# A state-space layer inside a four-layer kernel: two of its channel blocks convolved in the weights, its decay stage folded into its neighbours, and its decay rows made by one 32-row product a tile

## The reference

```python
zxbcdt = hn @ in_proj_w.T                      # (T, 644): z 256, xBC 384, dt 4
z, xBC = zxbcdt[:, :256], zxbcdt[:, 256:640]
dt = softplus(zxbcdt[:, 640:] + dt_bias)       # 4 heads
conv = conv_b + sum(pad(xBC)[k:k+T] * conv_w[:, k] for k in range(4))
x, B, Cc = split(silu(conv), (256, 64, 64))    # x: 4 heads of 64
dA = exp(dt * -exp(A_log))
state = state * dA_t + (dt_t * x_t) B_t        # per head, 64x64, over t
y_t = state C_t + D * x_t
out = rmsnorm(y * silu(z)) @ out_proj_w.T + residual
```

## Time and profile before

| | us |
|---|---|
| median of 3 runs | 5289.64 (5287.33 to 5296.65) |
| the profiled execution, its own time | 5287.22 |
| its span, first to last instruction | 5285.5 |
| outside the span | 1.7 |

### The profile page before, as it was taken

How to read it: one execution, slowest core, us unless ns; L and a number is a source line. 1 busy time by engine, 2 the same in 40 slices (tenths; PEclk the granted TensorE clock), 3 DMA queues, 4 the chain that set the end, 5 groups by cost and what they waited for, 6 DMA issues and landing times. The chain is left out here.

```text
span 5285.5 us, 74271 instructions
## 1 busy us (share of the span) xinstructions
PE 4229.8 (80%) x26784; PEld 2472.8 (47%) x26784; DVE 2894.0 (55%) x6283; ACT 2191.7 (41%) x4860; POOL 720.1 (14%) x780
## 2 busy tenths in 40 slices
PE   6787896798679789678777969968877786896887
PEld 3443234566444333456644433345664543334566
DVE  5554674454555476445455547644546554764454
ACT  3344464233334446323333544632333354463233
POOL 1100120310110112032011011203201101120320
PEclk8898897698789889779878988976987797897698
DMA  3101100100210111011021011101102101110110
GB/s 99 44 19 40 41 18 23 49 17 17 69 44 19 42 38 30 11 48 25 13 73 36 19 47 33 34 7 48 25 13 74 35 19 44 36 33 8 48 25 13
DMA packets 112338, 181.84 MB, mean 34 GB/s; under 512 B 25296, under 2 KB 63440, under 8 KB 109136
## 3 DMA queue, kind: packets, MB, share of 16 engines
q1 hardware_dynamic: 94480, 155.35, 10.7%
q10 hardware_dynamic: 17472, 21.51, 1.7%
HBM read 114.78 MB, written 27.26 MB: 27 GB/s over the span
## 5 line engine op out<-in xcount | busy, mean ns | idle before, releaser
L813 DVE TENSOR_REDUCE mhalf<-mx 128x1 f32<-128x512 f32 (+3 forms) x2064 | 1277.2, 654 | 734.6 <-PE mx L764 394.8
L786 ACT ACTIVATE prob<-ps_st 128x512 f32<-128x512 f32 (+3 forms) x2432 | 1116.9, 512 | 1296.9 <-PE ps_st L731 704.6
L761 PE MATMUL mx<-ks,qs 72*128 72x512 bf16 (+3 forms) x2304 | 847.1, 384 | 252.8 <-DVE mhalf L813 88.0
L728 PE MATMUL ps_st<-qs,ks 75*128 75x512 bf16 (+3 forms) x2432 | 751.8, 349 | 47.2 <-DMA qs<-neg 20.1
L761 PEld LDWEIGHTS mx<-ks,qs 72*128 72x128 bf16 x2304 | 233.7, 102 | 825.3 <-DVE mhalf L813 563.9
L711 PE MATMUL ps_o<-prob,vst 128*32 128x512 f32 (+3 forms) x5376 | 561.6, 501 | 0.3
L728 PEld LDWEIGHTS ps_st<-qs,ks 75*128 75x128 bf16 x2432 | 238.7, 100 | 273.4 <-ACT prob L786 142.5
L2241 ACT ACTIVATE pr<-ps,nm,lrq 128x192 f32<-128x192 f32 (+1 forms) x512 | 251.1, 502 | 239.3 <-DVE nm L2254 239.3
L2215 PE MATMUL po<-lv,ptr 128*128 128x64 f32 x1920 | 251.1, 285 | 5.6 <-DVE ptr L2266 5.6
L2215 PEld LDWEIGHTS po<-lv,ptr 128*128 128x128 f32 x1920 | 233.0, 198 | 37.2 <-DVE ptr L2266 30.2
L318 PE MATMUL turn<-table,nrm 128*128 128x128 f32 x224 | 63.6, 465 | 224.8 <-DVE nrm L297 224.8
(11 more groups left out here) (335 smaller groups left out, 7168.3 us busy)
## 6 DMA issues: line engine op xcount, KB each, us to landing
ks<-k_scr SPq DMA_DIRECT2D x144, 192.0 KB
qs<-q_scr SPq DMA_DIRECT2D x252, 96.0 KB
stream<-stream SPq DMA_DIRECT2D x16, 1152.0 KB, 9.8
k_scr<-ks SPq DMA_DIRECT2D x60, 192.0 KB
stream<-stream SPq DMA_DIRECT2D x16, 512.0 KB, 4.6
tabs<-local_tables SPq DMA_DIRECT2D x4, 2048.0 KB
lkt<-o SPq DMA_DIRECT2D x128, 64.0 KB, 2.1
lkt<-o ACTq DMA_DIRECT2D x128, 64.0 KB, 2.1
```

The lines of the kernel that those rows point to most:

```text
L728: last = nc.tensor.matmul(ps_st[:, u % 3, 0:q1 - q0], ks[g % 2][0:KR, h, kt * P:(kt + 1) * P], qs[g % 2][0:KR, hf, h, q0 - hf * HALF:q1 - ...
L761: last = nc.tensor.matmul(bank[:, j * w:(j + 1) * w], qs[g % 2][0:R, hf, h0 + j, (t - 4 * hf) * P:(t - 4 * hf + 1) * P], ks[g % 2][0:R, h0 ...
L786: nc.scalar.activation(prob[:, b % PROBS, h, 0:q1 - q0], ps_st[:, u % 3, 0:q1 - q0], ACT.Exp, scale=scale).then_inc(S["exped"], 1)
L813: nc.vector.tensor_reduce(mhalf[:, hf, h0:h0 + heads, t - 4 * hf, part], bank[:, 0:heads * (k1 - k0)].rearrange("p (n w) -> p n w", n=head ...
```

## The change

Nothing outside `mamba`, its packed weights and the constants changes. In the diff's order:

- The convolution of B and C (one block of 128 channels together) is put into the weights: POOL makes four scaled copies of their projection weights, one for each tap (wt), and PE accumulates four f32 products of 512 columns with shifted input columns for each half (`state_inputs`). ACT applies bias and silu straight from PSUM. C is moved to partitions 0 to 63 by a transfer. DVE convolves x's two halves only; the steps are interleaved with the small steps of dt.
- The phase m_decay is gone. Its sums are made on PE within m_proj, with one product more that gives the sums as 32 rows (4 heads of 8 tiles); DVE spreads these into a block-diagonal tile (`spread`). Its three small exponentials stand at the head of m_scan. xdt moves to POOL, one tile at a time; xw is made on DVE, one tile at a time, with dt folded into its weight.
- The decay rows of a tile are one f32 product of 32 rows and 512 columns and one bf16 mask product of 512 columns. DVE's subtraction is gone: ACT takes exp from PSUM with -cum as its bias, one instruction for each head. Decay rows are issued two tiles ahead.
- `keep_clock` issues products whose result nothing reads: three after each of the second half's four convolution steps, and ten between and behind the last turns of m_proj.

```diff
+    l3 += [("l3_cwr", np.concatenate([row(cw[256:, k]) for k in range(4)], 1)), ("l3_cbbc", cb[256:].reshape(-1, 1))]
...
+              ("own_tile", (q // 4 == np.arange(8)) * 1.0), ("own_head", (q % 4 == np.arange(4)) * 1.0),
...
+def keep_clock(net, bank, n):
+    for _ in range(n):
+        net.nc.tensor.matmul(bank, net.ident_bf, net.ident_bf.unsqueeze(1).broadcast_to([P, 4, P]), start=True, stop=True)
...
+                    sp.wait_ge(S["bc"], 2)
+                    sp.dma_start(c_ch[:, :], bc[N:P, :]).then_inc(S["c_moved"], 16)
...
+                    nc.gpsimd.tensor_tensor(wt[:, :, :], W("l3_xbc")[:, DI:DI + P].unsqueeze(1).broadcast_to([P, TAPS, P]),
+                                            W("l3_cwr").rearrange("p (k c) -> p k c", k=TAPS), ALU.mult).then_inc(S["taps"], 1)
...
+                    def state_inputs(i):
+                        pe.wait_ge(S["padded"], 3 + i)
+                        pe.wait_ge(S["taps"], 1)
+                        for k in reversed(range(TAPS)):
+                            a = max(0, TAPS - 1 - k - i * HALF)
+                            c0 = i * HALF + a - (TAPS - 1 - k)
+                            last = nc.tensor.matmul(pp[:, i, a:HALF], wt[:, k, :], net.in_ch[:, c0:c0 + HALF - a], start=(k == TAPS - 1),
+                                                    stop=(k == 0))
...
+                    pre(0)
+                    for t in range(NT):
+                        last = nc.tensor.matmul(p_dt[:, t, :], net.in_ch[:, t * P:(t + 1) * P], W("l3_dt"), start=True, stop=True)
+                    last.then_inc(S["dtmm"], 1)
+                    z(0)
+                    z(1)
+                    pre(1)
+                    z(2)
+                    z(3)
+                    for i in range(2):
+                        state_inputs(i)
+                    pe.wait_ge(S["step"], 9)
+                    flat = da[:, :, :].rearrange("p t h -> p (t h)")
+                    nc.tensor.matmul(pd[:, small:2 * small], net.K("tri"), flat, start=True, stop=True)
+                    nc.tensor.matmul(pd[:, 2 * small:3 * small], net.K("ones"), flat, start=True, stop=True)
+                    nc.tensor.matmul(p_rows, flat, net.K("tri"), start=True, stop=True).then_inc(S["cums"], 1)
+                    for t in range(4, NT):
+                        z(t)
+                    pe.wait_ge(S["bc"], 2)
+                    for i in range(2):
+                        turn(i, b_ch, N)
+                    for i in range(2):
+                        pe.wait_ge(S["silu"], i + 1)
+                        turn(2 + i, xs[:, 0, :], P)
+                    for k in range(5, 9):
+                        pe.wait_ge(S["conv"], k)
+                        keep_clock(net, spare[:, :], 3)
+                    for i in range(2):
+                        pe.wait_ge(S["silu"], 3 + i)
+                        turn(4 + i, xs[:, 1, :], P)
+                        keep_clock(net, spare[:, :], 2)
+                    keep_clock(net, spare[:, :], 4)
...
+                    nc.scalar.activation(na[:, :], W("l3_alog"), ACT.Exp).then_inc(S["nega"], 1)
+                    pads(0)
                     act.wait_ge(S["step"], 2)
                     nc.scalar.activation(e[:, :, :], e[:, :, :], ACT.Exp, scale=-1.0).then_inc(S["exp"], 1)
+                    pads(1)
                     act.wait_ge(S["step"], 3)
                     nc.scalar.activation(dt[:, :, :], v[:, :, :], ACT.Ln).then_inc(S["ln"], 1)
...
+                    conv(0, 3)
+                    conv(1, 0)
+                    conv(1, 1)
                     dve.wait_ge(S["cums"], 1)
+                    nc.vector.tensor_scalar(ncum[:, :, :], p_cum, -1.0, None, ALU.mult).then_inc(S["decay"], 1)
+                    nc.vector.tensor_copy(etot[:, :, :], p_tot).then_inc(S["decay"], 1)
+                    nc.vector.tensor_tensor(spread[:, :, :], p_rows.unsqueeze(1).broadcast_to([small, H, P]),
+                                            net.K("own_head")[0:small, :].unsqueeze(2).broadcast_to([small, H, P]), ALU.mult).then_inc(S["decay"], 1)
...
+                    conv(1, 2)
+                    for i in range(2):
+                        to_tok(i, b_tok[:, 4 * i:4 * i + 4, :], N)
+                    conv(1, 3)
...
+                    def inputs(t):
+                        nc.gpsimd.tensor_tensor(hd(xdt[:, t, :]), hd(x_tok[:, t, :]), wide(dt[:, t, :]), ALU.mult).then_inc(S["xdt"], 1)
...
-                        for h in range(H):
-                            nc.tensor.matmul(pr[:, t % 2, h, :], da[:, t, h:h + 1].broadcast_to([P, P]), net.K("tri"), start=True, stop=False)
-                            last = nc.tensor.matmul(pr[:, t % 2, h, :], net.ident_bf, net.later_kq, start=False, stop=True)
+                            pe.wait_ge(S["decay"], H * (t - 1))
+                        nc.tensor.matmul(pr[:, t % 2, :, :], net.K("own_tile")[0:NT * H, t:t + 1].broadcast_to([NT * H, P]), spread[:, :, :],
+                                         start=True, stop=False)
+                        nc.tensor.matmul(pr[:, t % 2, :, :], net.ident_bf, net.later_kq.unsqueeze(1).broadcast_to([P, H, P]), start=False,
+                                         stop=True).then_inc(S["rows"], 1)
...
+                        for h in range(H):
+                            nc.scalar.activation(ex[:, t % 2, h, :], pr[:, t % 2, h, :], ACT.Exp, bias=ncum[:, t, h:h + 1]).then_inc(S["decay"], 1)
...
+                    def weighted(t):
                         if t >= 2:
+                            dve.wait_ge(S["smm"], t - 1)
+                        nc.vector.tensor_tensor(hd(xw[:, t % 2, :]), hd(x_tok[:, t, :]), wide(wend[:, t, :]), ALU.mult).then_inc(S["xw"], 1)
```

More of the change, by code:

```diff
@@ L1559, in mamba @@
         da = kept("m_da", [P, NT, H])
-        with net.phase("m_proj", ["zero", "pre", "padded", "conv", "silu", "turned", "tok", "zmm", "z", "dtmm", "step", "exp", "ln", "nega"]) as (S, blk):
+        ncum = kept("m_ncum", [P, NT, H])
+        etot = kept("m_etot", [P, NT, H])
+        wend = kept("m_wend", [P, NT, H])
+        spread = kept("m_spread", [NT * H, H, P])
+        ss = kept("m_ss", [P, NT])
+        b_ch = bc[0:N, :]
+        with net.phase("m_proj", ["taps", "zero", "pre", "padded", "bcmm", "bc", "c_moved", "conv", "silu", "turned", "tok", "zmm", "z", "dtmm", "step",
+                                  "exp", "ln", "nega", "cums", "decay"]) as (S, blk):
             xp = net.tmp("xp", [P, 2, T + 3])
@@ L1571, in mamba @@
             pz = net.psum("pz", [P, 2, HALF])
[L1572 to L1588, removed]
+            pd = net.psum("pd", [P, HALF])
+            spare = net.psum("spare", [P, HALF])
+            small = NT * H
+            p_dt = pd[:, 0:small].rearrange("p (t h) -> p t h", h=H)
+            p_cum = pd[:, small:2 * small].rearrange("p (t h) -> p t h", h=H)
+            p_tot = pd[:, 2 * small:3 * small].rearrange("p (t h) -> p t h", h=H)
+            p_rows = pd[0:small, 3 * small:3 * small + P]
             with blk as block:
@@ L1608, in pre @@
+                            nc.tensor.matmul(pp[:, i, :], W("l3_xbc")[:, j * P:(j + 1) * P], net.in_ch[:, i * HALF:(i + 1) * HALF],
                                              start=True, stop=True).then_inc(S["pre"], 1)
[L1610 to L1620, removed]
@@ L1621, in _, with z @@
[L1621 to L1623 removed]
+                    def z(t):
+                        if t >= 4:
+                            pe.wait_ge(S["z"], t - 2 - t % 2)
+                        nc.tensor.matmul(pz[:, t // 2 % 2, t % 2 * DI:(t % 2 + 1) * DI], net.in_ch[:, t * P:(t + 1) * P],
+                                         W("l3_z"), start=True, stop=True).then_inc(S["zmm"], 1)
@@ L1624, in _, with turn @@
+                    def turn(k, src, m):
                         if k >= 2:
@@ L1651, in _ @@
-                    silu(act, 3)
+                    for t in range(4):
+                        gates(t)
+                    for i in range(2):
+                        act.wait_ge(S["bcmm"], i + 1)
+                        nc.scalar.activation(bc[:, i * HALF:(i + 1) * HALF], pp[:, i, :], ACT.Silu, bias=W("l3_cbbc")).then_inc(S["bc"], 1)
+                    silu(0)
+                    for t in range(4, NT):
+                        gates(t)
+                    silu(1)
                 @block.vector
@@ L1742, in mamba @@
-        with net.phase("m_scan", ["skip", "skipped", "gated", "sq", "rows", "diff", "decay", "gmm", "mt", "intra", "inter", "smm", "scaled", "state", "part", "y"]) as (S, blk):
+                    conv(0, 3)
+                    conv(1, 0)
+                    conv(1, 1)
+                    dve.wait_ge(S["cums"], 1)
+                    nc.vector.tensor_scalar(ncum[:, :, :], p_cum, -1.0, None, ALU.mult).then_inc(S["decay"], 1)
+                    nc.vector.tensor_copy(etot[:, :, :], p_tot).then_inc(S["decay"], 1)
@@ new lines, in _ @@
+                    conv(1, 3)
+                    for j in range(2):
```

(8 more changed lines are left out.)

188 lines of the change are left out of this document (82 added, 106 removed).

## The result

| | us |
|---|---|
| median before | 5293.15 (5287.33 to 5299.48, 4 runs) |
| median after | 5236.76 (5229.02 to 5250.91, 4 runs) |
| ratio | 0.9896, 95% interval 0.9871 to 0.9921 |
| profiled execution after, its own time and its span | 5229.02 and 5227.3 |

The change made the kernel faster, by 1.0%: 56 us, where 130 were forecast. The time lies in the range (5140 to 5265), which the rivals had widened, and 77 us from the predicted 5160: the forecast's own case did not happen.

A forecast was written before the change was run, and what follows sets the result against it. PE was taken to bound the scan. Per pass, scan -28.1, decay stage -6.9 and projection +2.5 gave -32.5; four passes -130, from 5287.2 to 5157, median 2.4 higher, so 5160 us; range 5140 to 5265.

The forecast's parts named there:

- the forecast's own case: Whole kernel: clock fast through the scan, 5160 us, own range 5140 to 5180, chance 0.48.
- the part on the clock: Scan: PE enters from unbroken keep_clock products, so the clock stays high through most of it; called the least certain step.
- The idle time ahead of the door: Change from projection to scan: PE idle some 0.7 us, after which the clock may be gone.
- The clock drops at the scan's door: Rival, scan start: clock lost at the 32-row products, scan 61 us, -7.5 a pass, 5260; chance 0.23.
- part of the way: Rival, scan: clock lost midway or in some passes; half the tiles at 7.25, -19.5 a pass, 5212; chance 0.22.
- The scan at 2.4 GHz: Scan: 4.0 us a tile, eight are 32, 4.0 for entry and tail, 36.0 against 64.1.
- DVE and POOL: Scan: they get in each other's way, DVE 3.15 to 4.15 us a tile, 0 to 1.2 us a scan.
- The main case's claim that PE stays the bound: Scan, per tile: DVE 2.55, ACT 2.1 and POOL 2.7 us all lie under PE's 4.0.
- The decay stage: m_decay, between projection and scan: gone as a phase, -6.9 us a pass.
- C's transfer: Projection: 256 KB starting near 21.5 us, needing less than 4.6, ending before 27 and costing nothing.
- The projection's +2.5: Projection: PE's order sums to 33.7 us against 31.2, +2.5 a pass; bounds 30 and 36.
- the twelve dummy products: Projection, keep_clock ahead of turn(4): 3.3 us with four starts, 2 to 3 us of the path.

The follow-up runs named there:

- e2: The changed kernel with the f32 decay product given 128 rows in place of 32, the added rows zeros; 5146.88 us, ratio 0.9729 to the kernel before.
- e5: The changed kernel with the f32 decay product given 64 rows in place of 32, the added rows zeros; 5147.1 us, ratio 0.9719 to the kernel before.
- e3: The changed kernel, 32 rows kept, plus three unread bf16 products of 128 rows and 384 columns in each tile's decay group; 5158.62 us, ratio 0.9766.
- e4: The changed kernel with the decay rows of the kernel before in place of the new ones, nothing else; 5146.17 us, ratio 0.9733.
- e8: The kernel before with keep_clock alone: ten products behind m_proj's last turn, twenty behind m_decay's sums; 5228.08 us, ratio 0.9881.
- e1: The changed kernel with all keep_clock products left out; 5235.05 us, ratio 0.9894 to the kernel before.
- e9: e5 with dt's products ahead of pre(0) on PE and dt's small steps ahead of convolution and copies; 5133.42 us, ratio 0.9708.
- e10: e5 (64 rows) without keep_clock; 5233.72 us, ratio 0.9905 to the kernel before.
- e7: e2 and e1 together: the changed kernel with 128 rows and no keep_clock; 5149.11 us, ratio 0.9723.
- e11: e7 (128 rows, no keep_clock) with dt's products first; 5202.85 us, ratio 0.9851 to the kernel before.

## Why the prediction was partly wrong

**The failed step** is in the part on the clock: "I take it that the clock stays high through most of the scan." It fell 2.5 us in, in three passes, and 11.5 us in, in one, and the scan took 60.2 and 52.8 us in place of 36.0. The cause is shown from both sides: it is the 32 rows of the decay product. Rows of zeros added to the same product (e2, e5) hold the clock; full-height work beside it (e3) holds it too, and the old rows (e4) do as well. The idle time ahead of the door, which the prediction named as a second suspect and put at 0.7 us, is 0.4 to 0.5 us in all of these. The prediction had priced 32 rows by their time and found no discount, which is right (1.09 us against 1.13), and noted that such products "stand in no row"; it did not let that decide the chances. Why few rows lose the clock is not shown, only that they do; e8's first pass shows that they are not the only thing that can.

**The rival that happened** is "The clock drops at the scan's door", in three passes, with "part of the way" in the first. It was priced at -7.5 a pass; those three passes gave -12.5 in the mean. The difference is in the projection (3.2), the output stage (1.0) and the scan (0.8). That the first pass rose early and kept the clock longer, which is worth 12 us of the profiled execution, was luck.

**The scan at 2.4 GHz** was right: tile 4.0 forecast, 3.93 in e2; scan 36.0 forecast, 36.0 in e2. This is shown for 128 rows; with 32 rows and nothing beside them no scan ran at that clock to its end. At 1.2 GHz the tile was 7.25 forecast and 7.35 measured; the scan 61 against 60.2.

**DVE and POOL** meet as forecast: sdec 0.41 us alone and 0.94 under POOL's multiplication in e2, xw 0.42 and 0.65. In the tile shown sdec ends at 2191.61, 0.27 us behind POOL, though it had begun 0.67 us ahead of POOL's end. In e2's trace each of the 44 sdec and xw instructions that begin under a POOL instruction ends 0.27 to 0.28 us behind it, whenever it began, so DVE waits for POOL's end, with perhaps the first 0.13 of its 0.41 us done before (an estimate from these two numbers). That is the stronger form that the Trainium skill ("SBUF — State Buffer", "SBUF: two separate sides") has, and the trace agrees. It cost nothing, since PE's steps alone fill the pitch; DVE was busy 24.26 us in the scan, 3.03 a tile. The main case's claim that PE stays the bound holds.

**The decay stage** is gone, as forecast: -6.9. C's transfer landed in 3.0 us and held nothing up.

**The projection's +2.5 was mis-sized**: measured -0.6 (31.1 to 30.5). The rise came at 12.5 us, as by the sum (12.7); the products ahead of it took 12.1 us, and state_inputs 6.9 where 7.1 stood. The later terms were too dear by their group starts: z(4) to z(7) 1.9 us for 2.5, four turns 2.0 for 2.4, the twelve dummy products 2.6 for 3.3, the last turns and their dummy products 2.8 for 3.5. Of this last 0.7, an estimated 0.4 is a miscount: the sum has ten products there, the code eight, and 0.215 us stood for one. The dummy products as a whole cost 1.4 of the path (e1), where 2 to 3 were named for the twelve alone.

**Not forecast:** the output stage's -1.0; it has the same work at a higher clock (0.69 against 0.63). The change has no share in it that a run shows: with the same output code it took 11.5 to 13.1 us in the traces (e2, e3). And that e9's order saves 1.7 us in most passes: the sum simply took all before the end of pre(1) at 1.2 GHz, and did not ask what the new place of dt's products did to the rise, which lay 9 us in before and 12.5 after.

**What stays open:** why the clock rises 3.5 us into some projections and 12.5 into others of the same instructions (e2: one pass of four; in the changed kernel the first pass). The traces tie it to something ahead of the projection: in all nine passes with an early rise, of the 52 in the thirteen traces, the clock had last fallen 17.0 or 17.1 us ahead of the projection's first product, and in the other 43 passes 14.3 to 15.0 us ahead. No edit here controlled it, and a part of each total hangs on it.

## What to carry to other kernels

When a product is made with fewer rows, its own time hardly changes, but the work around it may lose the fast clock, and here that was 24 us on top of a scan of 36. Padding it to 64 or 128 rows with zeros costs next to nothing, so try it. Before a forecast rests on a clock, ask which instructions stand in the first microseconds behind a phase change, and compare them in height and columns with stretches of the trace in which the clock held or fell. Measure an idea like `keep_clock` on the old algorithm too: it gave 26.5 us in three passes of four, where the rewrite was to give 32.5 a pass, and 63 us in the median, about as much as the rewrite as it stood (56) and less than half of the rewrite with 128 rows (e2, 149).

## What the runs showed of the hardware that I had not expected

- PE recorded busy 2.00 of 2.00 us does not hold the clock: it fell in such a stretch (clock 0.72) with 32-row products. Padding to 64 or 128 rows, all zeros, held it in every pass of e2, e5 and e9 at no cost in the product's time. On that time these runs agree with the Trainium skill ("TensorE: Matmul & The Clock Gate", "Why this matters for your kernels"), which has a single product of 32 rows take as long as one of 128; by starts the 32-row pair took 1.06 us here, 0.09 more than the one of 128.
- Holding was easier than raising: 64 rows held the clock (e5), and did not raise it in 60 us (e10); with 128 rows it rose 4.2 us in (e7, three passes) or 6.8 (e7, the first), or 20 and 51 us in (e11), and in the scan of the kernel before never.
- DVE waits out a POOL instruction: of sdec and xw, whose two inputs lie in SBUF, each one that began under a POOL instruction ended 0.27 to 0.28 us behind it (e2, 44 cases).
- One kernel's passes and runs can differ by more than an edit is worth: e8's runs lie at 5209 to 5212 and at 5244, and its scans, in the one run with a trace, at 37.6 and 62.3 us. A median over a few runs of such a kernel says little; the stages say more.
